# Vision tower kernel: token stage on pairs of 64-row matrix tiles, the last two heads' steps in another order, and one power moved from GpSimd to ScalarE

## What is computed

```python
# 1 token stage, per image; d_gamma is one 1024 x 1024 matrix for all
q, k, v = x @ Wq + bq, x @ Wk + bk, x @ Wv + bv
y = ((d_gamma * (q @ k.T)) @ v) @ Wo + bo
h = where(y >= 0, y, prelu_a * y)
# 2 attention, 8 heads of width 8, bias by relative position
h = h + attention(layernorm(h))
# 3 mixture of 8 experts, top 2 of a router, GELU
h = h + experts(layernorm(h))
```

## Time and profile before

| | |
|---|---|
| time, median of 3 runs | 642.88 us (642.76 to 647.92) |
| the profiled execution, its own time | 644.97 us |
| its span, first to last instruction | 643.2 us |
| PE busy | 579.1 us (90%) |
| DVE busy | 461.6 us (72%) |
| ACT busy | 360.5 us (56%) |
| POOL busy | 85.1 us (13%) |
| PE clock granted, mean | 0.934 of full speed |

### The profile page before, as it was taken

How to read it: one execution, slowest core, us unless ns; L and a number is a source line. 1 busy time by engine, 2 the same in 40 slices (tenths; PEclk the granted TensorE clock), 3 DMA queues, 4 the chain that set the end, 5 groups by cost and what they waited for, 6 DMA issues and landing times.

```text
span 643.2 us, 12871 instructions
## 1 busy us (share of the span) xinstructions
PE 579.1 (90%) x4160; PEld 185.7 (29%) x4160; DVE 461.6 (72%) x554; ACT 360.5 (56%) x633; POOL 85.1 (13%) x197
## 2 busy tenths in 40 slices
PE   8999989884789999999999999999998884799996
PEld 4322322221212223222322223222322631233221
DVE  4456344547688999999999999999997344455844
ACT  2101312111248888888898888888897244244443
POOL 9502001012001000100001010110101342011100
PEclk9999899997559999999999999999999588699999
DMA  8300372405332232323232232323233000000001
GB/s 291 99 4 0 100 206 46 131 5 159 73 93 76 69 82 66 92 59 90 70 73 76 68 83 60 93 62 83 73 85 107 10 10 28 13 6 17 17 0 34
DMA packets 50611, 45.16 MB, mean 70 GB/s; under 512 B 26165, under 2 KB 38806, under 8 KB 50582
## 3 DMA queue, kind: packets, MB, share of 16 engines
q1 hardware_dynamic: 50582, 44.78, 25.2%
HBM read 28.59 MB, written 16.17 MB: 70 GB/s over the span
## 4 chain that ended last, share of the span: by engine, by line
PE 76%; DVE 10%; issue 6%; ACT 5%; POOL 2%; ACTq 1%; DVEq 0%; POOLq 0%
PE ps L1283 19%; PE ps L1268 12%; PE ps L1161 8%; PE ps L1178 8%; PE ps L1171 5%; PE ps L1416 5%; PE ps L1442 4%; ACT probs L716 3%; DVE nmax L852 2%; PE ps L1298 2%; PE ps L1234 1%; PE ps L1100 1%; PE ps L1272 1%; PE ps L1192 1%; PE ps L1133 1%
## 5 line engine op out<-in xcount | busy, mean ns | idle before, releaser
L852 DVE TENSOR_REDUCE nmax<-ps 128x1 f32<-128x1024 f32 x256 | 301.7, 1217 | 33.4 <-PE ps L1178 24.5
L716 ACT ACTIVATE probs<-ps 128x512 f32<-128x512 f32 x512 | 277.9, 597 | 66.5 <-PE ps L1268 56.7
L1283 PE MATMUL ps<-probs,v_ring 128*32 128x256 f32 x2048 | 167.4, 400 | 0.0
L1268 PE MATMUL ps<-q_ring,k_ring 51*128 51x512 bf16 x512 | 105.2, 392 | 13.8 <-ACT probs L716 13.8
L1178 PE MATMUL ps<-k_ring,q_ring 48*128 48x512 bf16 x512 | 104.1, 396 | 11.4 <-DVE nmax L852 11.4
L1161 PE MATMUL ps<-g_t,x_rows 96*128 96x512 f32 x128 | 64.7, 623 | 5.2 <-DVE gated L875 5.2
L1268 PEld LDWEIGHTS ps<-q_ring,k_ring 51*128 51x128 bf16 x512 | 30.8, 94 | 124.9 <-issue 83.4
L1283 PEld LDWEIGHTS ps<-probs,v_ring 128*32 128x32 f32 x2048 | 40.8, 109 | 88.4 <-ACT probs L716 47.5
L733 ACT ACTIVATE probs<-ps,wide_w 128x1024 f32<-128x1024 f32 x32 | 35.5, 1113 | 51.5 <-PE ps L1416 50.1
L875 DVE TENSOR_TENSOR gated<-ps,gamma_sb 128x512 f32<-128x512 f32 x64 | 42.5, 686 | 25.6 <-PE ps L1161 25.5
L1083 DVE TENSOR_TENSOR probs<-probs,ps 128x1024 f32<-128x1024 f32 x32 | 39.1, 1221 | 29.9 <-PE ps L1429 26.7
(11 more groups left out here) (158 smaller groups left out, 375.6 us busy)
## 6 DMA issues: line engine op xcount, KB each, us to landing
k_ring<-qk_parts SPq DMA_DIRECT2D x64, 96.0 KB, 2.4
q_ring<-qk_parts SPq DMA_DIRECT2D x64, 96.0 KB, 2.4
gamma_sb<-gamma_t SPq DMA_DIRECT2D x4, 1024.0 KB, 10.0
v_padded<-v_pad SPq DMA_DIRECT2D x4, 1024.0 KB, 4.6
v_ring<-v_padded SPq DMA_DIRECT2D x32, 128.0 KB, 3.2
outputs<-o_t SPq DMA_DIRECT2D x32, 128.0 KB
qk_parts<-qk_h SPq DMA_DIRECT2D x8, 384.0 KB, 4.4
x_ring<-bias_parts SPq DMA_DIRECT2D x32, 96.0 KB, 3.0
```

What stands on the lines that cost most here:

```text
L716: A.activation(probs[:, s % 4, HALF * j:HALF * (j + 1)], ps[:, key_bank(s, j), :], ACT.Exp).then_inc(exp_done[j], 1)
L852: V.tensor_reduce(nmax[:, par, s:s + 1], ps[:, bank:bank + 2, :].rearrange("p a n -> p (a n)"), AX, ALU.max, negate=True).then_inc(s1_redu ...
L1268: last = mm(ps[:, key_bank(s, j), :], k_ring[rows, u, P * s:P * (s + 1)], q_ring[rows, u, HALF * j:HALF * (j + 1)], start=True, stop=not c ...
L1283: last = mm(ps[VC * j:VC * (j + 1), PVB, 0:2 * P], v_ring[:, u, m, :], probs[:, m % 4, 2 * P * j:2 * P * (j + 1)], start=(m == 0), stop=(m ...
```

## The change

- **Token stage in full steps.** Weights are no longer folded to 65 rows. `x_rows` holds each image twice, in partitions 0 to 63 and 64 to 127, and `k_t`, `q_t` likewise; biases are added by ACT on the copy out (`Identity` with a bias). `score` now issues two matmuls of 64 rows, one on the upper and one on the lower half of the array, for the two halves of the columns. The gate covers 128 x 1,024 in one instruction. `retain` issues the same two matmuls as before. The gate has two double banks (0-1, 2-3) and two buffers where there were three banks and four buffers.
- **Values** are projected straight into token rows by 8 matmuls of 64 columns on alternating row halves, so `turn_v` is gone; DVE adds their bias as it copies (`leave_v`). The attention values (`project_vv`) go the same way, and copy straight to `v_pad`. Normed rows are turned 4 at a time by 128 columns instead of 8 by 64.
- **Order.** The sums of batch n are turned in batch n + 1 as before, but its normed rows, its query/key and value projections and their parts move to batch n + 2. The fifth pass is replaced by a written-out sequence that finishes batches 2 and 3 among the first 16 score tiles. ACT's order per batch is: sum, normed rows, high part, middle part, values, then k and q of the next batch, then the square.
- **Loads.** x and the token weights are loaded twice over (two halves of the partitions); the attention weights too, with the bias row apart.
- **Last attention pass.** `load_sums` goes ahead of the operand loads of u = 0, `invert_sums` from step (1, 1) to (0, 5), `store_inverse` to the end of u = 0, `load_inverse` ahead of the maxima's rows of u = 1. The table `WITHIN` is moved by one or two steps; `turn_logits(0)` goes behind the last values, ahead of `up(0)`.
- **Gap.** For batches 0 to 2, ACT does `Exp` of the gap before the first GELU, in place of POOL's power. Batch 3 stays on POOL.

```diff
 # PE, token stage
-            def score(at): ...
-                mm(ps[:, at % 3, :], x_all[:, T * b + P * s:T * b + P * (s + 1)],
-                   g_t[:, b % 2, HALF * j:HALF * (j + 1)], start=True, stop=True).then_inc(tok_scored, 1)
+            def score(at):
+                b, s = at // NT, at % NT
+                if s == 0:
+                    pe.wait_ge(k_copied, b + 1)
+                    pe.wait_ge(q_copied, b + 1)
+                if at >= 2:
+                    pe.wait_ge(tok_gated, at - 1)
+                for j in range(2):
+                    rows = slice(D * j, D * (j + 1))
+                    last = mm(ps[:, 2 * (s % 2) + j, :], k_t[rows, b % 2, P * s:P * (s + 1)], q_t[rows, b % 2, :],
+                              start=True, stop=True)
+                last.then_inc(tok_scored, 1)
+            def project_v(b):          # project_vv is alike, from hn_t and qkv_w
+                pe.wait_ge(k_copied, b + 1)
+                for c in range(NT // 2):
+                    for j in range(2):
+                        last = mm(ps[:, 5 + j, D * c:D * (c + 1)], x_half(b, j)[:, P * c:P * (c + 1)],
+                                  wvo[D * j:D * (j + 1), :], start=True, stop=True)
+            for b in range(B):
+                for s in range(NT):
+                    at = b * NT + s
+                    retain(at)
+                    if at + 2 < B * NT:
+                        score(at + 2)
+                    if b >= 2 and s == 0:
+                        turn_hn(b - 2)
+                    if b >= 2 and s == 1:
+                        project_qk(b - 2)
+                    if b >= 1 and s == 2:
+                        turn_y(b - 1)
+                    if b >= 2 and s == 3:
+                        project_vv(b - 2)
+                    if b + 1 < B and s == 4:
+                        project_k(b + 1)
+                    if b + 1 < B and s == 5:
+                        project_q(b + 1)
+                    if b + 1 < B and s == 6:
+                        project_v(b + 1)
+                    if b == 0 and s == 6:
+                        turn_bias()
+                    if b == 0 and s == 7:
+                        spread_bias()
+            turn_y(B - 1)
+            first_scores(0, 2)
+            turn_hn(B - 2)
+            first_scores(2, 3)
+            project_qk(B - 2)
+            first_scores(3, 4)
+            project_vv(B - 2)
+            first_scores(4, 6)
+            turn_hn(B - 1)
+            first_scores(6, 7)
+            project_qk(B - 1)
+            first_scores(7, 8)
+            project_vv(B - 1)
+            first_scores(8, 2 * NT)
 # DVE, token stage
+            leave_v(0)
+            for b in range(B):
+                for s in range(NT):
+                    gate(b, s)
+                    if b == 0 and s == 5:
+                        small_tables()
+                    if b >= 2 and s == 2:
+                        rest_part(b - 2)
+                    if b >= 2 and s == 3:
+                        low_part(b - 2)
+                    if b >= 1 and s == 4:
+                        activate(b - 1)
+                    if b >= 1 and s == 5:
+                        first_center(b - 1)
+                    if b >= 1 and s == 6:
+                        norm_var(b - 1)
+                    if b + 1 < B and s == NT - 1:
+                        leave_v(b + 1)
+                    if b >= 1 and s == NT - 1:
+                        norm_scale(b - 1)
+            activate(B - 1)
+            first_center(B - 1)
+            first_maxima(0, 1)
+            rest_part(B - 2)
+            first_maxima(1, 2)
+            norm_var(B - 1)
+            low_part(B - 2)
+            first_maxima(2, 3)
+            norm_scale(B - 1)
+            first_maxima(3, 5)
+            rest_part(B - 1)
+            first_maxima(5, 7)
+            low_part(B - 1)
+            first_maxima(7, 8)
+            turn_maxima(0, 0, None)
+            first_maxima(8, 2 * NT)
 # ACT
+            for b in range(B):
+                if b >= 1:
+                    leave_ret(b - 1)
+                if b >= 2:
+                    leave_hn(b - 2)
+                    high_part(b - 2)
+                    middle_part(b - 2)
+                    leave_vv(b - 2)
+                if b + 1 < B:
+                    leave_k(b + 1)
+                    leave_q(b + 1)
...
+                if b >= 1:
+                    square(b - 1)
+            leave_ret(B - 1)
+            square(B - 1)
+            for n in (B - 2, B - 1):
+                leave_hn(n)
+                high_part(n)
+                middle_part(n)
+                leave_vv(n)
...
+            act.wait_ge(gap_ready, 1)
+            A.activation(e_gap[:, TILES[0]], gap[:, TILES[0]], ACT.Exp).then_inc(e_gap_ready, 1)
 # PE, last attention pass
-            WITHIN = {(2, 1): [(project_attention, 0)], (2, 2): [(project_attention, 1)],
-                      (2, 4): [(project_attention, 2)], (2, 6): [(turn_norm, 0)], (3, 0): [(turn_norm, 1)],
-                      (3, 3): [(turn_norm, 2), (logits, 0), (logits, 1)], (3, 5): [(logits, 2)], (3, 7): [(turn_logits, 0)]}
+            WITHIN = {(2, 2): [(project_attention, 0)], (2, 3): [(project_attention, 1)],
+                      (2, 5): [(project_attention, 2)], (3, 0): [(turn_norm, 0)], (3, 2): [(turn_norm, 1), (logits, 0)],
+                      (3, 5): [(turn_norm, 2), (logits, 1)], (3, 7): [(logits, 2)]}
```

More of the change, by code:

```diff
@@ L449, in attend_sp @@
                     loads = not (first and u == 0) and not (last and u > 0)
+                    if last and u == 0:
+                        for i in range(2):
+                            sp.wait_ge(o_stored[i], 16 * (G - NH) // 2 + 1)
+                        for b in range(B - 1):
+                            load_sums(b)
+                    if last and u == 1:
+                        for b in range(B - 1):
+                            load_inverse(b)
                     if loads:
@@ L796, in _ @@
             V.memset(qk_scale[D:P, :], 1.0).then_inc(tables_ready, 1)
-            for b in range(1, B):
-                V.memset(x_all[D:KX, T * b:T * (b + 1)], 1.0).then_inc(x_ones, 1)
             for e in range(E):
@@ new lines, in gate @@
+            def gate(b, s):
+                at = b * NT + s
+                if b == 0 and s % 2 == 0:
+                    dve.wait_ge(gamma_loaded[s // 2], 16)
+                dve.wait_ge(tok_scored, at + 1)
+                if at >= 2:
+                    dve.wait_ge(tok_summed, at - 1)
+                V.tensor_tensor(gated[:, s % 2, :], ps[:, 2 * (s % 2):2 * (s % 2) + 2, :].rearrange("p a n -> p (a n)"),
+                                gamma_sb[:, s, :], ALU.mult).then_inc(tok_gated, 1)
@@ new lines, in first_maxima @@
+            def first_maxima(a, z):
+                for i in range(a, z):
+                    row_max(i // NT, i % NT, i // NT)
+            activate(B - 1)
[10 more added lines that the diff above has]
+            first_maxima(5, 7)
@@ L1114, in warm @@
                 for _ in range(times):
[L1115 removed]
+                    mm(ps[:, 2, 0:P], zero[:, 0:P], zero[:, 0:P], start=True, stop=True)
             pe.wait_ge(warm_ready, 1)
@@ L1141, in turn_v, with project_q @@
-            def turn_v(b):
-                pe.wait_ge(vt_copied, b + 1)
+                    last = mm(ps[:, 5 + j, :], wk_d[D * j:D * (j + 1), :], x_half(b, j), start=True, stop=True)
+                last.then_inc(k_projected, 1)
+            def project_q(b):
                 if b >= 2:
                     pe.wait_ge(y_read, b - 1)
-                turn_four(7, vt_s, v_turned)
+                for j in range(2):
+                    last = mm(ps[D * j:D * (j + 1), 7, :], wq_d[D * j:D * (j + 1), :], x_half(b, j), start=True, stop=True)
+                last.then_inc(q_projected, 1)
@@ L1170, in retain, with turn_y @@
                 pe.wait_ge(tok_gated, at + 1)
-                mm(ps[D * j:D * (j + 1), 3, :], v_s[:, b % 2, s, :], gated[:, at % 4, :], start=(s == 0),
-                   stop=(s == NT - 1)).then_inc(tok_summed, 1)
+                for j in range(2):
+                    last = mm(ps[D * j:D * (j + 1), 4, :], v_s[:, b % 2, s, :], gated[:, s % 2, HALF * j:HALF * (j + 1)],
+                              start=(s == 0), stop=(s == NT - 1))
+                last.then_inc(tok_summed, 1)
+            def turn_y(n):
+                pe.wait_ge(ret_copied, n + 1)
+                if n == 0:
+                    pe.wait_ge(bias_kept, 1)
+                if 1 <= n < B - 1:
+                    pe.wait_ge(hn_t_copied, n)
+                if n == B - 1:
+                    pe.wait_ge(y_read, n)
+                turn_four(7, ret_t, y_turned)
@@ new lines, in turn_hn @@
+            def turn_hn(n):
+                pe.wait_ge(hn_ready, n + 1)
+                pe.wait_ge(q_copied, min(n + 2, B - 1) + 1)
+                if n == B - 2:
+                    pe.wait_ge(y_read, B)
+                if n == B - 1:
```

(24 more changed lines are left out.)

420 lines of the change are left out of this document (169 added, 251 removed).

## The result

The changed kernel takes 623.28 us (median of four, 619.25 to 627.10), the kernel before 644.13 in the same series: a ratio of 0.966, interval 0.959 to 0.973. I had forecast 596 us and a range of 584 to 618. The sign was right, and less than half of the gain came. Medians are over all executions, ratios and intervals leave out those over 1.5% above the fastest of the same kernel, and a kernel for which no ratio is given was executed once.

A forecast was written before the change was run, and what follows sets the result against it. PE was taken to bound the token stage, and a chain the way on to the first exponential. Profiled 645.0 - 35.4 (attention begins earlier) - 8.0 (last pass) - 3.8 (gap) = 597.8, so 596 us in the median; range 584 to 618.

The forecast's parts named there:

- The loads: Loads before the last gamma tile: 0.6 MB more, 2 us at 268 GB/s, with the last tile wanted only at 26 us.
- The start: Time until PE's first sum in the token stage: 13.5 us, with 1.5 either way, against 13.6 before.
- The steps: Token stage on PE: score pair 0.96 us plus sums 1.01, so 1.97 a step instead of 2.93.
- Values and attention values: PE's value projections in the token stage: 5 times 16 records at 0.14, 2.2 us a time, 11.0 together.
- The waits: PE's waits in the token stage, 9.1 us together: rest part 1.3 twice, batch turn 1.8 twice, bias copies, tables, last steps.
- The tail: Last sum to first exponential: two batches finished in series on DVE, PE at half clock, 39.2 us.
- The last pass: Last attention pass: earlier inversion removes PE's 4.2 us wait and the half clock after it; -8.0 us net.
- The end gives little: Rival for the last attention pass: only 1 of the 8.0 us gain is left, time 603 us; 10%.
- The gap: Between attention and experts: DVE's 4.28 us wait for POOL's power becomes one ACT instruction, -3.8 us, table load covered.
- More waits than worked out: Rival for the token stage: waits from ACT's fixed order put 19 of its 84 us at half clock, 615 us; 15%.
- Pairs do not overlap: Rival for PE's row-half pairs: 44 pairs at 1.92 instead of 0.96 us, time 638 us; 5%.
- half clock throughout: Rival for the token stage: PE's 84 us become 168 at half clock, time 680 us; 3%.

The follow-up runs named there:

- e1: The changed kernel with every load that fills both partition halves split into two DMAs of 64 rows: 602.42 us, ratio 0.928.
- e8: e1 with gamma's first two tiles loaded as 2 by 64 rows, no row read twice: 621.08 us.
- e9: The changed kernel with the doubled loads still one DMA each, but row first and copy second (64 by 2): 598.86 us.
- e5: e1 with the small bias copy `bv_b` made by ACT instead of DVE: 602.43 us, ratio 0.935.
- e11: e1 once more, the same instructions: 602.98 us, ratio 0.935.
- e4: e1 with the matmuls of `project_v` and `project_vv` run through one row half and then the other, instead of alternating: 604.38 us.
- e6: e1 with the gap of batches 0 to 2 back on POOL's power instead of ACT: 609.50 us.
- e10: e5 with DVE's first maxima moved ahead of the rest parts in the tail, and PE's ninth score tile ahead of batch 3's values: 599.53 us, ratio 0.932.
- e7: e1 with the last attention pass in its old places (SP's loads, inversion, projections, turns of norm and logits): 605.33 us.
- e3: e1 with both matmuls of a score reading rows 0 to 63, so on one row half of the array: 619.45 us.

## Why the prediction was wrong, point by point

**The loads: the step that failed.** It stood as "The loads before the last gamma tile grow by 0.6 MB, 2 us at 268 GB/s, but the last tile is wanted only at 26 us". I priced bytes at the rate of rows 1 and didn't ask whether loads of another form have that rate. The third of four gamma loads came at 39.5 us. The form cost 20.4 us up to the start of attention, shown by e1, e8 and e9. The bytes were counted rightly (two images and the token weights once more are 0.6 MB), and e9 moves the same bytes without harm. In profiled time e1, without the form, is still 5.5 over my sum: 4.4 at the start, 0.5 in the tail and 1.1 behind it, less 0.5 in the stage.

**The start.** Without that form the first sum still came at 18.05, not at 13.6 ± 1.5. Of these 4.4 us, up to 2.0 are DVE's copy of the bias column, which my sum didn't name (e5). Another 1.7 are the projections of k and q on a PE at half speed: 3.7 us in e1 (10.21 to 13.90), where the same two take 1.96 later. The rest of 0.7 has no row of its own. How much early work runs at half speed changes from kernel to kernel, and between e1 and e11, one kernel, the first sum moved by 0.8.

**The steps.** Right in kind, a little off in size. The kernel after, PE's timeline:

```profile
27.87 1.08 PE L1241 MATMUL ps<-gated,v_s 128*64 128x512 f32 x4 [0.63 <-DVE gated L882]
28.88 1.13 PE L1230 MATMUL ps<-q_t,k_t 64*128 64x512 f32 x4
29.94 1.08 PE L1241 MATMUL ps<-gated,v_s 128*64 128x512 f32 x4
```

A step takes 2.07 (27.87 to 29.94), not 1.97, since a score pair followed by sums takes 1.06, not 0.96. Eleven of the thirty pairs in the stage stand ahead of matmuls of their own form, 64 rows by 128 columns, and keep 0.96; the other 19 cost 0.1 more each, 1.9 us. Here the prediction also misread its rows: the experts' pair of 0.96 stands ahead of `spread`, which has that same form, so these rows held no change from a row pair straight to the sums. A drain at that change would fit the 0.1, but isn't shown: a projection of k ahead of sums takes 0.95 (70.76 to 71.71 in the kernel after). Values and attention values were mis-sized the other way: 0.93 for 16 records, not 2.2, some 6 us in all. I had taken the rate from matmuls whose row halves don't alternate; e4 shows 0.5 of the 1.27 to be the order, and part of the rest is that I divided the length of the records, 1.93, instead of the 1.66 from their start to the next matmul's. Together PE's work came to 81.9 for 84.0.

**The waits.** 10.7 us in e1 against 9.1. In the kernel after, the rest part costs 1.01 each time (forecast 1.3), the turn of a batch 2.11 and 2.03 (forecast 1.8). Behind such a turn PE can run at half speed for two pairs, which my sum had only as a rival:

```profile
82.27 1.98 PE L1241 MATMUL ps<-gated,v_s 128*64 128x512 f32 x4 [2.11 <-DVE gated L882]
84.17 1.75 PE L1230 MATMUL ps<-q_t,k_t 64*128 64x512 f32 x4
```

It costs 1.5 us there. In e1 two single pairs took 1.67; in e6, after waits of 2.10 and 2.03, four pairs took 1.87 to 1.98, and its stage 95.1. The stage's 92.6 for 93.1 is thus partly luck: steps, values, waits and clock were each off, and the errors cancel.

**The tail.** 39.7 for 39.2, in after and in e1 alike, with the clock at 0.57. That it goes by DVE's order was in the sum, but I took that order for given; e10 shows 8 us in it.

**The last pass.** Forecast -8.0; against e7, e1 has -4.3, and the kernel after, which kept its full clock longer, ran 9.8 shorter than e7. ACT's wait of 7.73 went in the kernel after, where no idle time of ACT in this part is over 2.3; in e1 two of 4.3 stand, at a clock of 0.50, so 5.5 us there hang on how long the clock stays low, which isn't settled. Head 30's rows came 0.89 us late (forecast 1.0). Turning the logits behind the last values costs 2.0 as forecast (3.95 us from the last copy to the gap's exponential in e7, 5.92 in e1). "The end gives little", 1 of the 8.0, is out.

**The gap.** -3.98 for -3.8; the table load stays hidden.

**The rivals.** "More waits than worked out", at 615, came nearest in time but not in kind: its waits were to come from ACT's order, and they came from SP's queue. "Pairs do not overlap" is refuted by e3, "half clock throughout" by 0.93. No rival of mine was about the loads. And the profiled execution, 619.25, was the fastest of four: from own time to median I had taken 2.1 off, where 4.0 had to be added.

## What to carry to other kernels

Price a load by its shape as well as its bytes: look at the first dimension of what a changed DMA reads and writes, and don't leave a 2 there. With rows first (64 or 128 here) the loads were quick, even as two DMAs for one. When a change makes an early stage a third faster, list every load that the stage waits for and when it lands, and SP's issue times with them, before counting matmuls. Where two chains alternate on one engine, look for the engine's long waits and put independent work ahead of them; here it shortened the tail by 8 us.

## What the runs showed of the hardware

- A load with a first dimension of 2 moves about 50 GB/s on 0.13 of the DMA engines, measured in 43 to 48 us of the kernel after. Over the first 19.5 us all loads together move at 146 GB/s with this form, 236 with two DMAs each and 323 with the row first. The form also holds up SP: 12.8 us for the issue of two plain loads behind it, 1.1 in e1.
- A DVE copy of 64 by 128 elements took 1.47 to 3.04 us beside POOL's memsets and always ended with one of them; on ACT it took 0.31.
- Sixteen fp32 matmuls of 64 by 64 take 0.93 us when row halves alternate, 1.43 when one half follows the other.
- In the last pass the two profiled executions of one kernel agree within 0.3 us, and kernels with the same instructions there differ by up to 5.8; between e1 and the kernel after it is how long the granted clock stays at 0.5. What decides that stays open.
